# Router logits in four column strips, V in plain float32, and batch 2's first steps two steps later

## The reference, cut to what matters

```python
x = x + ssm(layernorm(x))      # conv, silu, scan over 512 tokens, output projection
x = x + ffn(layernorm(x))      # 8 experts, all of them computed for every token
x = x + attention(layernorm(x))
x = x + ffn(layernorm(x))

def ffn(x):
    router_probs = softmax(einsum('bsh,he->bse', x, w_router))
    gate_weights = softmax(einsum('bsh,he->bse', x, w_gating) / 0.1)
    h = silu(einsum('bsh,ehf->ebsf', x, w_gate)) * einsum('bsh,ehf->ebsf', x, w_up)
    expert_out = einsum('ebsf,efh->ebsh', h, w_down)
    cw = router_probs * gate_weights
    cw = cw / (sum(cw, -1) + 1e-9)
    return einsum('ebsh,bse->bsh', expert_out, cw)

def attention(x):              # q, k and v are x @ W.T + b, v among them
    ...
```

## Time and profile before

| | before |
|---|---|
| median of 3 runs | 1431.55 us (1431.43 to 1433.21) |
| the profiled execution's own time | 1431.87 us |
| span in the profile, first to last instruction | 1429.9 us |
| TensorE busy | 1372.5 us (96% of the span), 12348 matmul records |
| VectorE busy | 950.6 us (66%) |
| ScalarE busy | 769.4 us (54%) |
| GpSimdE busy | 515.7 us (36%) |

### The profile page before, as it was taken

The page is one execution under the profiler, slowest core; times in us unless marked ns, Lnnn a source line. Parts: engine busy times, 40 slices in busy tenths (PEclk is TensorE's granted clock), DMA queues, the critical chain, the costliest instruction groups (busy, mean ns, idle before and its releaser), DMA issues.

```text
span 1429.9 us, 30749 instructions
## 1 busy us (share of the span) xinstructions
PE 1372.5 (96%) x12348; PEld 1193.3 (83%) x12348; DVE 950.6 (66%) x2295; ACT 769.4 (54%) x1041; POOL 515.7 (36%) x517
## 2 busy tenths in 40 slices
PE   4889999999999999999999989999999999999998
PEld 3788878888788888888888878888888888888887
DVE  7665677775876668568675776657856665576543
ACT  6564748553565556637465665456634563365321
POOL 4260654433423453247312751236403421341000
PEclk9899999999999999999999999999999999999999
DMA  7110231003010310121003200050003000300000
GB/s 238 49 36 17 80 66 32 26 6 78 2 47 16 74 21 1 47 67 34 10 1 83 64 1 9 1 116 31 2 1 71 9 2 1 71 9 2 8 1 8
DMA packets 70233, 51.35 MB, mean 36 GB/s; under 512 B 4140, under 2 KB 60508, under 8 KB 70092
## 3 DMA queue, kind: packets, MB, share of 16 engines
q1 hardware_dynamic: 70060, 49.38, 14.2%
q10 hardware_dynamic: 32, 0.02, 0.0%
HBM read 44.92 MB, written 4.46 MB: 35 GB/s over the span
## 4 chain that ended last, share of the span: by engine, by line
PE 79%; DVE 7%; POOL 4%; issue 4%; ACT 3%; DVEq 0%; POOLq 0%
PE pd L1123 26%; PE pg L287 8%; PE pu L287 7%; PE pg L289 7%; PE pg L288 7%; PE pu L288 7%; PE pu L289 7%; PE att_ps L764 2%; POOL arena L709 2%; PE att_ps L789 2%; DVE h L1232 1%; POOL arena L711 1%; DVE x L1220 1%; PE pd L1115 1%; PE side_ps L339 1%
## 5 line engine op out<-in xcount | busy, mean ns | idle before, releaser
L1183 ACT ACTIVATE h<-pg 128x512 f32<-128x512 f32 x512 | 304.3, 598 | 615.9 <-PE pg L289 613.4
L1123 PEld LDWEIGHTS pd<-w_down,h 128*128 128x128 f32 x3840 | 482.6, 192 | 33.3 <-issue 3.5
L1123 PE MATMUL pd<-w_down,h 128*128 128x128 f32 x3840 | 488.8, 275 | 1.1 <-DVE x L1220 1.1
L1232 DVE TENSOR_TENSOR h<-h,pu 128x512 f32<-128x512 f32 x512 | 344.9, 678 | 213.8 <-PE pu L289 203.2
L287 PE MATMUL pg<-ffn_x_hi,w_gate_hi 128*128 128x512 f32 (+1 forms) x544 | 248.1, 456 | 1.1 <-DVE ffn_x_lo L372 1.1
L287 PE MATMUL pu<-ffn_x_hi,w_up_hi 128*128 128x512 f32 (+1 forms) x544 | 210.3, 387 | 10.2 <-DVE h L1232 10.1
L289 PE MATMUL pg<-ffn_x_hi,w_gate_lo 128*128 128x512 f32 (+1 forms) x544 | 208.5, 383 | 0.0
L288 PE MATMUL pg<-ffn_x_lo,w_gate_hi 128*128 128x512 f32 (+1 forms) x544 | 208.5, 383 | 0.0
L288 PE MATMUL pu<-ffn_x_lo,w_up_hi 128*128 128x512 f32 (+1 forms) x544 | 208.5, 383 | 0.0
L289 PE MATMUL pu<-ffn_x_hi,w_up_lo 128*128 128x512 f32 (+1 forms) x544 | 208.2, 383 | 0.0
L974 POOL TENSOR_TENSOR att_arena<-att_arena,r_sums 128x512 f32<-128x512 f32 (+1 forms) x72 | 72.4, 1006 | 273.0 <-DVE r_sums L854 272.9
(11 more groups left out here) (226 smaller groups left out, 1512.3 us busy)
## 6 DMA issues: line engine op xcount, KB each, us to landing
arena<-bc_spread SPq DMA_DIRECT2D x56, 256.0 KB, 4.5
att_arena<-v_rows SPq DMA_DIRECT2D x64, 144.0 KB, 3.8
att_arena<-v_rows SPq DMA_DIRECT2D x64, 128.0 KB, 3.7
arena<-in_x SPq DMA_DIRECT2D x8, 256.0 KB, 2.9
x<-in_x SPq DMA_DIRECT2D x8, 256.0 KB, 3.1
w_down<-in_w_down SPq DMA_DIRECT2D x8, 256.0 KB, 4.8
v_rows<-att_arena SPq DMA_DIRECT2D x8, 256.0 KB, 2.3
out<-x SPq DMA_DIRECT2D x8, 256.0 KB, 2.2
```

The lines of the kernel that those rows point to most:

```text
L1123: last = nc.tensor.matmul(pd[:, t * P:(t + 1) * P], h_b[:, d % NH, t * P:(t + 1) * P], wd[:, d % NCH, :], start=d % CPE == 0 and t == 0, s ...
L1183: nc.scalar.activation(h_b[:, c % NH, :], pg[c % 2][:, :], ACT.Silu).then_inc(gate_done, 1)
L1232: nc.vector.tensor_tensor(h, h, pu[d % 2][:, :], ALU.mult).then_inc(h_done, 1)
```

## The change

Three things change, apart from one another.

**The router.** Instead of 128 tokens as weights, each matmul takes 32 tokens and writes 32 partitions of the bank; four of them, one per column strip of the array, make a tile. 64 matmuls become 256.

**V.** V is one plain float32 matmul for each tile, from a float32 copy `axf` of the transposed rows that ScalarE now makes too (a second copy of the bank, which also frees it). The low part is now computed from `axf` in SBUF, and Q waits for that low part by a semaphore of its own, `x_lo`. `w_v` is kept in one copy, not in two parts.

**The table.** The steps of the state-space layer of batch 2 are put 2 chunks later (`st`, `rows`, `dt`), 2.5 or 2.6 (`win`, `ln`), 1.5 (`k`) and 1 (`y`).

```diff
@@ _ssm_slots
     if i == 2:
-        return dict(st=24, rows=25.5, ln=26, win=28.5, dt=32, k=(36, 39, 42, 45), y=50.5)
+        return dict(st=26, rows=27.5, ln=28.6, win=31, dt=34, k=(37.5, 40.5, 43.5, 46.5), y=51.5)
@@ build
-        wv = [sb(f"w_v_{v}", [P, P], F32R) for v in ("hi", "lo")]
+        wv = sb("w_v", [P, P])
...
+        axf = q_room[:, 1, :]
@@ Head.pe
                 for t in range(a, z):
-                    last = nc.tensor.matmul(ps[:, t * 2 * E:(t + 1) * 2 * E], fx[m % 2][:, t * P:(t + 1) * P],
-                                            pk("w_route"), start=True, stop=True)
+                    for s in range(0, P, 32):
+                        last = nc.tensor.matmul(ps[s:s + 32, t * 2 * E:(t + 1) * 2 * E],
+                                                fx[m % 2][:, t * P + s:t * P + s + 32], pk("w_route"), start=True, stop=True)
@@ Att.pe
-                ab.wait_free(pe, ("ln3", j))
+                pe.wait_ge(x_lo, j + 1)
...
                 for t in range(TT):
-                    out, xw = ps[:, t * P:(t + 1) * P], [a[:, t * P:(t + 1) * P] for a in (axh, axl)]
-                    nc.tensor.matmul(out, xw[0], wv[0][:, :], start=True, stop=False)
-                    nc.tensor.matmul(out, xw[1], wv[0][:, :], start=False, stop=False)
-                    last = nc.tensor.matmul(out, xw[0], wv[1][:, :], start=False, stop=True)
+                    last = nc.tensor.matmul(ps[:, t * P:(t + 1) * P], axf[:, t * P:(t + 1) * P], wv[:, :],
+                                            start=True, stop=True)
@@ Att.act
                 nc.scalar.copy(axh[:, 0:L], ab.ps(("ln3", j))[:, :]).then_inc(x_hi, 1)
+                ab.free(nc.scalar.copy(axf, ab.ps(("ln3", j))[:, :]), ("ln3", j))
@@ Att.dve
-                dve.wait_ge(x_hi, j + 1)
-                ab.free(nc.vector.tensor_tensor(axl[:, 0:L], ab.ps(("ln3", j))[:, :], axh[:, 0:L].bitcast(F32),
-                                               ALU.subtract), ("ln3", j))
+                ab.wait_free(dve, ("ln3", j))
+                nc.vector.tensor_tensor(axl[:, 0:L], axf, axh[:, 0:L].bitcast(F32), ALU.subtract).then_inc(x_lo, 1)
@@ small_weights, VectorE
-                    link(nc.vector.tensor_copy(wv[0][:, :], pk("w_v")))
-                    nc.vector.tensor_tensor(wv[1][:, :], pk("w_v"), wv[0][:, :].bitcast(F32), ALU.subtract).then_inc(w_small, 1)
+                    nc.vector.tensor_copy(wv[:, :], pk("w_v")).then_inc(w_small, 1)
```

More of the change, by code:

```diff
@@ L220, in build @@
         y_part, y_done, bc_moved = sem("y_part"), sem("y_done"), [sem("bc_moved0"), sem("bc_moved1")]
-        x_hi = sem("x_hi")
+        x_hi, x_lo = sem("x_hi"), sem("x_lo")
         v_zero, v_pad, v_out, v_moved, p_t = sem("v_zero"), sem("v_pad"), sem("v_out"), [sem(f"v_moved{i}") for i in range(2)], sem("p_t")
```

## The result

| | before | changed kernel |
|---|---|---|
| median (5 runs each, same chip) | 1431.55 us (1430.75 to 1433.21) | 1423.76 us (1422.09 to 1425.63) |
| ratio | | 0.9946, interval 0.9932 to 0.996 |
| the profiled execution | 1431.87 us, span 1429.9 | 1425.63 us, span 1423.8 |

The changed kernel is 7.8 us faster; forecast were 8.9. Its profiled execution is the slowest of its five, 1.9 us above its median. One later execution of the kernel before (1929 us, mean granted clock 0.66) and one of an experiment (1453 us, 0.91) ran in a slow state and are left out everywhere.

The account below looks back on a forecast made before the run. TensorE's queue, busy 96%, was taken to set the end. Router 5.1, V 3.5, start 0.3 and table 0.8 make 9.7 us, less 0.8 waited away: 8.9 us, forecast 1422.7 us, range 1418 to 1428.5 us.

Parts of the forecast that it names:

- V, 3.5 us: V's matmuls on TensorE: twelve records become eight, piece 1.80 to 1.36 us, 0.44 us less for each of 8 batches.
- The router, 5.1 us, with 0.8 waited away: Router's piece 1.35 to 1.05 us at 15 full heads, plus hidden mode changes; 0.8 us of all savings lost to waits.
- The 0.15 us extra for the hidden change of mode: At four router heads where TensorE waits anyway, the wait hides the array's mode change: an estimated 0.15 us more saved each.
- Rival 1: Router strips give nothing, since a floor under each matmul makes 32 narrow records cost eight wide ones: 1427.3 us; chance 0.09.
- Rival 4: Router strips run one after the other, each record as dear as a full one: 39.6 us more, 1467 us; chance 0.03.
- The second copy, at no cost: ScalarE's 8 extra copies, 4.6 us, delay Q nowhere: cost nothing; without the cover 5 us.
- The table, a gain of 0.8 us: Batch 2's moved steps: four TensorE waits shrink or go, new ones come; gain 0.8 us, bounds 5.1 gain to 3.3 loss.
- the bank wait of 1.68: Batch 2's projection waits 1.68 us for the bank pass 1's head holds; claimed to shrink to some 0.2 us.
- the new one for `xs_lo`: Batch 2: `xs_lo` ends after TensorE reaches `dt`, a new wait of 1.4 us where there was none.
- the clip's: Up product's 0.56 us wait for the `h` behind line 558's clip, which waits for ScalarE; claimed to grow to about 1.9 us.
- up to 0.9 us ahead of an up product and 0.9 us ahead of batch 2's `y`: Possible new TensorE waits around batch 2's scans, up to 0.9 us each, counted against the 1.19 us wait that should go.
- Rivals 2 and 3: Batch 2's table: 2, new waits worse, loss 3.3 us, 1426.8 us, chance 0.13; 3, all four waits go, 1418.4 us, 0.09.

Follow-up runs that it names:

- the last one: Changed kernel with batch 1's `y` one chunk later on TensorE and batch 2's scans half a chunk earlier: 1420.21 us, ratio 0.9917.

## Why the prediction was right, and where it was not

- **V, 3.5 us.** The piece came out at 1.36 us, as read from the down product. On the way it pays 0.45 us at seven batches. Batch 0's share depends on the table: with the new one 0.2 us are kept, with the old one 1.6 us are lost. The fit gives 2.7 ± 0.35 us for V and its 0.3 us at the start, where 3.8 were forecast.
- **The router, 5.1 us, with 0.8 waited away.** The piece is right to 0.02 us. At three heads the whole saving is waited away at the next late `h` or value product, at two more most of it: of 6.1 us that the heads bring in the trace 2.2 are lost, where I had 0.8 for all parts. That leaves 3.9 us by the steps of the trace, and 3.9 ± 0.35 us by the fit. The 0.15 us extra for the hidden change of mode is in the trace (0.5 us in place of 0.32 at the four heads with a wait ahead, and also at three without one), but two of the four keep nothing and one 0.2 us.
- **Rival 1**, the floor under narrow matmuls, is out: 9 ns a record, by the doubled router. The section "Wait — 56ns, not 53.3ns?" of the Trainium skill's page "TensorE: Matmul & The Clock Gate" puts it at about 25 ns; the runs here don't agree with it for records that go round the four strips. **Rival 4** is out with it: the piece got shorter.
- **The second copy, at no cost**: right, and even a third costs nothing in the trace.
- **The table, a gain of 0.8 us, is the step that failed**: beside the kernel before its waits cost 1.2 us, beside router and V with the old table 0.4 us, and by the fit it is 0.4 ± 0.35 us slower. Of its parts, the bank wait of 1.68 (0.2, measured 0.26, now ahead of the transposes), that of B and C (0.2, measured none), the new one for `xs_lo` (1.4, measured 1.25) and the vanished 1.19 were right; the clip's was 1.9 and is 1.22. What went wrong are the "up to 0.9 us ahead of an up product and 0.9 us ahead of batch 2's `y`", which are 2.01 and 1.50, and which I then didn't count in full. With them the prediction's own laying was 3.7 + 0.9 + 0.9 = 5.5 us of waits against 5.1 before, a loss of 0.4 us; the gain of 0.8 does not follow from it. I had laid the durations as they stood before: the norm with 1.41 us. In its new place it runs beside a POOL product and takes 2.49. 0.9 + 1.1 is the 2.0 us measured. What V does to the old table's last wait I had not laid either.
- **Rivals 2 and 3** were the two ends of the table. The old waits did shrink, so the loss is 1.2 us of waits and not 3.3. But a stretch at 1.2 GHz did come behind the new wait of 2.01 us, as rival 2 has it, though that wait is far shorter than the 3.3 us that rival 2 named. It is 3.4 us long and in the profiled executions of all six kernels with the new table and batch 1's `y` in its old place; in the changed kernel:

```profile
159.20:163.00 3.80, 3.78 (x16) 3.44 (x17) 3.77 (x5) 1.07 (x2) 1.62 (x2) 0.57 0.01 4
```

- **The sum.** By the fit the parts are 3.9 + 2.7 - 0.4 = 6.2 us, and the slightly higher mean clock of the changed kernel's runs (0.9932 against 0.9927) is 0.3 more: 6.5 us, where I had 8.9. The whole was measured at 7.8, with an interval of 5.7 to 9.7 us. So the forecast time is right within what can be measured, but its closeness is in part luck: each of the three parts came out below its forecast, by 0.4 us (router, with the 0.8 taken off it), 1.1 (V) and 1.2 (table), and the share of router and V together that stays unexplained made up for it. The prediction also said that it is wrong if the number of stretches at 1.2 GHz changes. Between chunk 24 and the last one it did in the profiled executions, from three (6.8, 3.4 and 3.4 us) to four (3.4 us each); their sum, 13.6 us, did not, so that the 6.2 us between these two executions owe little to the clock. That the stretches can hide or feign the table's share was the right caution: table and clock could only be told apart chunk by chunk.

## What to carry to other kernels

A saving on the engine that sets the end is worth its size only up to the next wait that another engine ends: follow each saving in the trace to the first wait behind it, and count it there. When steps are moved, a duration does not move with them: look at what will run beside it. Where the granted clock differs from run to run, single parts of 2 us can't be told by a median of five runs; compare the start of the same chunk in two traces, and runs at equal mean clock.

## What the hardware showed unexpectedly

- 32 plain float32 records with 32 weight columns and 16 moving, round the four strips, take 0.30 us in all, 9 ns each; a record with 128 x 128 weights takes 110 ns.
- The four tensor_scalar of the norm take 1.11 us on VectorE alone (six of eight batches of the changed kernel), 2.49 us where a POOL tensor_tensor of 1.30 us begins 0.17 us after them, and 1.37 us beside a POOL tensor_scalar. The difference of 1.38 us is close to that product's length. Batch 1's norm takes 3.17 us beside two such products of 1.28 us each, 2.06 us more than alone. The Trainium skill's page "SBUF — State Buffer", section "SBUF: two separate sides", says that VectorE, in a mode that uses both ports or with two inputs from SBUF, and GpSimd take turns on a shared pair of ports, one blocked while the other holds it. Which mode the norm runs in, no run here shows; the 2.49 us agree with that rule, the 3.17 us and the 1.37 us beside the tensor_scalar only in part.
- The clock behind a wait: with 3.3 us ahead of batch 1's `y`, the profiled executions of eight of ten kernels have a stretch of 3.4 to 6.8 us at 1.2 GHz there and two have none; with the wait at 1.96 us, none of four has. Two windows of the same length over it, of the kernel before and of the last one:

```profile
106.50:114.50 8.00, 7.29 (x39) 7.32 (x40) 4.57 (x16) 1.20 (x2) 0.89 (x2) 0.58 0.23 68
```

```profile
106.50:114.50 8.00, 7.59 (x67) 7.62 (x68) 7.87 (x31) 1.49 (x3) 2.55 (x4) 1.00 0.23 68
```

What decides between the eight and the two stays open: the wait is the same to 0.1 us. Nor does the length of the wait decide: behind waits of 1.93 to 2.01 us for `h`, at 159 to 163 or at 180 us, eight profiled executions have a stretch of 3.4 us and three (the ones with batch 1's `y` later) have none.
